# A fused attention and feed-forward kernel on one core: load order, one VectorE swap, and the weight preparations of fc, w2 and b2 on other queue places and engines

## The chip, the core and the metric

The kernel runs on 1 core of one Trainium2 chip. The metric is the time on the device in microseconds (us), the median of several runs. The engines of the core work from queues of their own, in order, and wait for one another by semaphores: TensorE (PE, and PEld for its weight loads), VectorE (DVE), ScalarE (ACT), GpSimd (POOL) and SyncE (SP, which only starts DMA transfers here).

## The reference

For x of 2 batches x 2048 rows x 128 columns, float32:

```python
x = x + layernorm(attn(layernorm(x)))
x = x + layernorm(ffn(layernorm(x)))

def attn(h):                        # one head of width 128
    q, k = rope(bf16(h @ Wq.T)), rope(bf16(h @ Wk.T))
    e = where(causal, exp(q @ k.T / sqrt(128)), 0)
    o = e.sum(-1)                   # one number for each row, no values
    return relu(o[..., None] @ fc1_w.T + fc1_b) @ fc2_w.T + fc2_b   # 1 -> 16 -> 128

def ffn(h):                         # 16 experts; the gates are constant
    ...                             # gate 1 holds all the weight
    return relu(h @ W1[1] + b1[1]) @ W2[1] + b2[1]                  # 128 -> 256 -> 128
```

## The kernel before

The 4096 rows are 8 groups of 512 (4 tiles of 128 rows), group 0 to 3 of batch 0, 4 to 7 of batch 1. The front (first layernorm, q, k, rope) runs over nine units: unit 0 and 1 are the halves of group 0, unit 2 is group 1, unit 3 is group 4, unit 4 is group 5, unit 5 is group 2, 6 is group 6, 7 is group 3, 8 is group 7. The middle (scores, exponentials, attention's net, first residual, hidden layer) and the output have units of a similar kind.

The whole schedule is written out by hand in one text, `STEPS`. Each word is a step with its unit, an engine letter where there is a choice (A ScalarE, D VectorE, P GpSimd) and after # the banks of PSUM that it uses. Each engine walks the text and does its own steps in that order, so a step that waits holds up all the steps behind it on the same engine. A bank can be written again only when the step that empties it is done. The steps that matter here:

- `load_*` on SyncE's queue (L331 for x, L312 for the weights of q and k, L314 to L316 the three transfers of fc, L322 w2).
- `stat1.n` on VectorE (L642, bn_stats, two tiles in one instruction), `eps1.n` (variance plus epsilon; L357 on VectorE and GpSimd, L614 on ScalarE), `rstd1.n` on GpSimd (a power, L505), `norm1.n` (rows times rstd, L351), `tr1.n` on TensorE (transposes, L727), `+tr1.n` (copy of the bank to SBUF, L521).
- `wqk.0` (L710) centers the weights of q and k by a matmul, `+wqk.0` takes them to SBUF; `q.n`, `k.n` on TensorE (L735), `+q.n`, `+k.n` the copies to bf16 (L521).
- `swap.n`: two transfers (L339, L340) that exchange the halves of q and k for the rotation; units 0 and 1 use a matmul `rot.n` (L745) instead. `cos.n`, `sin.n` (L386, L383 on GpSimd, L410 from PSUM), `rope.n` (L420): products and the sum, most on VectorE.
- `scores.b.j.s` (L761, masks L765), `exp.b.j.s` on ScalarE with the row sum (L569), `sum.b` (L367), `hT.b` (L772), `+hT.b` (L538), `fc2.b` (L789).
- Weights: `fc.0` copies attention's net over the partitions by two pairs of matmuls (L717, L718); `fcmean.0` (L574, L575) and `+fc.0` (L579) on ScalarE take off each row's mean; `fcspread.0` on GpSimd (L472, L476) makes the block form by two selects. `w2mean.0` (L584) and `w2.0` (L590) do the same for the output's weights W2, `b2mean.0` (L594) and `b2.0` (L598) for b2. fc2.2 needs fcspread, the y steps (L810) need w2, and the splitting of b2 needs b2.

Of the kernel before, what the change touches and what calls it, by code (L numbers as in the profile page):

```python
# [38 lines left out]
load_x.3 blank.9#7 blank.1.256#7 load_x.0 repeat.0 load_x.4 mask.0 load_wqk.0 load_fc.0 stat1.3 load_x.1 stat1.0  # L39
eps1.3.P load_x.6 eps1.0.D stat1.4 rstd1.0 wqk.0#0 load_x.2 rstd1.3 eps1.4.A norm1.0.D load_x.8 tr1.0#1 fc.0#2  # L40
+wqk.0.A rstd1.4 load_w2.0 stat1.1 +tr1.0.A norm1.3.D eps1.1.A load_x.5 fcmean.0 k.0#1 rstd1.1 norm1.4.D tr1.3#0
load_x.7 +fc.0 q.0#3 norm1.1.D +tr1.3.A load_table.1 fcspread.0 stat1.6 tr1.4#2 tr1.1#4 load_table.4 stat1.2 +tr1.4.A
q.3#0 load_b1.0 +tr1.1.A stat1.8 +k.0.A k.3#2 w2mean.0 load_table.0 eps1.6.D stat1.5 rstd1.6 +q.3.A k.1#1 load_table.2
load_b2.0 stat1.7 eps1.8.A k.4#4 +k.3.A rstd1.8 norm1.6.D +q.0.A swap.3 q.4#0 eps1.2.A +k.4.A rstd1.2 norm1.8.D
tr1.6#3 +q.4.A load_table.3 cos.3.D rot.0#4 tr1.8#2 +tr1.6.A swap.4 norm1.2.D q.1#0 +tr1.8.A q.6#3 cos.4.D eps1.5.A
w2.0 b2mean.0 b2.0 sin.3.D tr1.2#2 +k.1.A rstd1.5 k.6#5 rope.3.D +q.6.A +tr1.2.A cos.0.D scores.2.2.0#3 eps1.7.A
sin.0.D scores.2.3.0#1 exp.2.2.0 k.8#2 rstd1.7 sin.4.D exp.2.3.0 scores.2.0.0#3 rope.0.D scores.2.1.0#4 +k.6.A q.8#6
rope.4.D exp.2.1.0 swap.6 norm1.5.D +k.8.A k.2#5 exp.2.0.0 cos.6.D +q.8.A scores.3.2.0#12 sum.2.D +q.1.A
scores.0.1.0#3 cos.8.D swap.8 scores.3.3.0#67 exp.0.1.0 cos.1.P +k.2.D rot.1#0 exp.3.2.0 tr1.5#4 sin.1.D q.2#3
exp.3.3.0 +tr1.5.D norm1.7.P hT.2#0 scores.3.1.0#12 +q.2.D scores.3.0.0#45 +hT.2 sin.6.D q.5#6 exp.3.1.0 swap.2  # L50
rope.1.D scores.0.0.0#0 exp.3.0.0 rope.6.D scores.0.3.0#1 load_w1.0 fc2.2#23 exp.0.0.0 sin.8.D exp.0.3.0
scores.5.0.0#45 cos.2.D +q.5.A scores.5.3.0#01 rope.8.D exp.5.0.0 k.5#7 stat3.2.D scores.0.2.0#6 exp.5.3.0 sin.2.D
# [798 lines left out]
```

## Time and profile before

| | |
|---|---|
| time of three runs | 91.88 us median, 91.78 to 91.89 |
| the profiled execution | 91.72 us, of which the span of the instructions is 90.0 us |
| busy share of the span | PE 92%, PEld 55%, DVE 85%, ACT 79%, POOL 63% |
| chain that ended last, by engine | PE 67%, ACT 20%, DMA 4%, POOL 2% |
| granted TensorE clock, mean | 0.997 |

The profile is of one execution. Busy shares are averages over stages of different kinds; a matmul's record overlaps the next one's, so a busy PE is not one at its peak. The chain is followed back from the last instruction: at each step to what released it or to the instruction before it on its engine. A timeline row shows start, duration, engine, line, operation, result and inputs, count, and in brackets the idle time before it and what ended it.

### The profile page before, as it was taken

What the parts mean: (1) busy time and instruction counts of PE and PEld (TensorE: products, weight loads), DVE (VectorE), ACT (ScalarE), POOL (GpSimd) and SP (SyncE); (2) the same over time, 40 slices, a digit from 0 to 9 for tenths busy, and PEclk for the clock granted to TensorE, in tenths of its full rate; (3) what the DMA queues carried; (4) which work ended last, traced back from release to release, by engine and by line L of the source; (5) the groups of instructions that cost most, each with busy time, mean ns of one, the idle gap of its engine ahead of it and who ended that gap; (6) DMA issues with size and microseconds to landing.
All of it is one profiled execution on the core that took longest, in us unless ns stands there. A gap on an engine that the chain in (4) does not pass through costs nothing.

```text
span 90.0 us, 1535 instructions
## 1 busy us (share of the span) xinstructions
...
## 2 busy tenths in 40 slices
...
GB/s 26 244 240 277 312 294 170 205 15 87 149 63 123 0 117 0 60 60 0 0 0 7 0 0 0 0 0 0 53 64 11 0 120 0 0 25 149 179 246 101
DMA packets 11900, 7.64 MB, mean 85 GB/s; under 512 B 867, under 2 KB 10996, under 8 KB 11892
## 3 DMA queue, kind: packets, MB, share of 16 engines
...
q8 instruction: 3, 0.05, 0.2%
...
## 4 chain that ended last, share of the span: by engine, by line
PE 67%; ACT 20%; DMA 4%; POOL 2%; SPq 2%; issue 1%; POOLq 1%; DVE 0%
PE psum L735 24%; ACT psum L569 15%; PE psum L810 15%; PE psum L761 12%; PE psum L727 7%; DMA wqk_f<-wqk_t 4%; PE psum L789 3%; POOL rstd L505 2%; SPq L331 2%; PE psum L781 1%; ACT qk L521 1%; PE psum L710 1%; PE psum L765 1%; PE psum L772 1%; PE psum L800 1%
## 5 line engine op out<-in xcount | busy, mean ns | idle before, releaser
L505 POOL TENSOR_TENSOR rstd<-ve,half_neg 128x4 f32<-128x4 f32 (+2 forms) x38 | 34.8, 925 | 13.8 <-DVE ve L357 9.6
L569 ACT ACTIVATE psum<-psum 128x1024 f32<-128x1024 f32 (+7 forms) x48 | 36.7, 764 | 1.4 <-PE psum L761 0.6
L761 PE MATMUL psum<-qk_r 128*128 128x512 bf16 (+3 forms) x80 | 20.7, 349 | 1.4 <-ACT psum L569 0.6
L810 PEld LDWEIGHTS psum<-w_c,hid 128*128 128x128 f32 x128 | 15.6, 192 | 1.3 <-DVE cols_n L521 0.4
L735 PE MATMUL psum<-cols_n,wqk 128*128 128x512 f32 (+1 forms) x36 | 16.1, 556 | 0.0
L810 PE MATMUL psum<-w_c,hid 128*128 128x128 f32 x128 | 16.1, 278 | 0.0
L735 PE MATMUL psum<-cols_n,w_c 128*128 128x512 f32 (+1 forms) x36 | 15.6, 552 | 0.0
L761 PEld LDWEIGHTS psum<-qk_r 128*128 128x128 bf16 x80 | 6.6, 97 | 12.9 <-ACT psum L569 6.4
L727 PE MATMUL psum<-ident,rows_n 128*128 128x128 f32 x64 | 10.2, 277 | 0.1
L357 POOL TENSOR_SCALAR ve<-stats 128x4 f32<-128x4 f32 (+2 forms) x9 | 2.1, 233 | 11.6 <-DVE stats L642 6.6
L727 PEld LDWEIGHTS psum<-ident,rows_n 128*128 128x128 f32 x64 | 7.2, 141 | 3.8 <-issue 1.6
L614 ACT ACTIVATE ve<-stats,small 128x4 f32<-128x4 f32 (+1 forms) x12 | 3.6, 301 | 7.1 <-DVE stats L642 6.0
L569 ACT ACTIVATION_READ_ACCUMULATOR psum<-psum 128x1 f32 x48 | 9.2, 192 | 0.0
L675 DVE SCALAR_TENSOR_TENSOR x<-psum,rstd,x_s 128x128 f32<-128x128 f32 x32 | 9.0, 342 | 0.2
L642 DVE BATCH_NORM_STATS2 stats<-x_s 128x6 f32<-128x256 f32 x16 | 5.8, 418 | 3.5 <-DMA x_s<-x 3.5
L649 DVE BATCH_NORM_STATS2 stats<-psum 128x6 f32<-128x256 f32 x21 | 8.0, 420 | 0.8 <-PE psum L810 0.5
L621 ACT ACTIVATE rows_n<-psum 128x128 f32<-128x128 f32 x22 | 5.8, 278 | 3.2 <-PE psum L810 2.3
L735 PEld LDWEIGHTS psum<-cols_n,w_c 128*128 128x128 f32 x36 | 6.2, 191 | 3.6 <-issue 2.0
L383 POOL TENSOR_TENSOR qk_r<-qk,table 128x512 bf16<-128x512 bf16 (+1 forms) x6 | 6.1, 1043 | 2.5 <-issue 2.5
L735 PEld LDWEIGHTS psum<-cols_n,wqk 128*128 128x128 f32 x36 | 6.0, 190 | 2.4 <-issue 1.1
L521 ACT ACTIVATE cols_n<-psum 128x512 f32<-128x512 f32 (+1 forms) x11 | 5.8, 538 | 1.8 <-PE psum L727 1.5
L521 ACT ACTIVATE qk<-psum 128x512 bf16<-128x512 f32 (+1 forms) x13 | 6.6, 536 | 0.3 <-PE psum L735 0.3
...
## 6 DMA issues: line engine op xcount, KB each, us to landing
...
```

Of the source, the lines that this page charges most:

```text
L383: last = eng.tensor_tensor(dst[:, g, i, c], src[:, g, i, c], table[:, kind, t0:t0 + w], ALU.mult)
L505: ready[k].done(eng.tensor_tensor(rstd[:, g, STAT_SLOT[k], t], ve[:, g, STAT_SLOT[k], t], half_neg[:, 0:tiles], ALU.pow), n)
L521: return eng.activation(dst, src, ACT.Copy) if on_act else eng.tensor_copy(dst, src)
L569: exps.done(eng.activation(area, area, ACT.Exp, scale=scale_qk, accum_out=sums[:, g, s, j:j + 1]), n, j, s)
L621: ins = eng.activation(rows_n[:, g, j0 + j, :], area, ACT.Square, accum_out=squares(g, k, slice(j0 + j, j0 + j + 1)))
L642: ins = eng.bn_stats(pair_stats(g, k, j), source[:, g, j:j + 2, :].rearrange("p t c -> p c t"))
L649: ins = eng.bn_stats(pair_stats(g, k, j0 + j), net_pair(k, n, j))
L675: ins = eng.scalar_tensor_tensor(dst[:, g, j0 + j, :], area, rstd[:, g, STAT_SLOT[k], j0 + j:j0 + j + 1], prev[:, g, j0 + j, :], ALU.mult, ...
L727: mm = eng.transpose(bank[:, j * P:(j + 1) * P], rows_n[:, g, j0 + j, :], ident[:, :])
L735: made[name].done(eng.matmul(bank_of(name, n)[:, 0:tiles * P], weight, cols_n[:, g, c], start=True, stop=True), n)
L761: mm = eng.matmul(psum[:, own[0] + i, 0:width], query, qk_r[:, g0 + c, 1, 0:width], start=True, stop=c < gb)
L810: mm = eng.matmul(bank[:, j * P:(j + 1) * P], hid[:, g, h, (j0 + j) * P:(j0 + j + 1) * P], w2_c[:, h, :], start=not seeded and h == 0, sto ...
```

## The change

In engine order it does this:

- SyncE: `load_wqk` is third, ahead of `load_x.4`, instead of fourth; `load_fc` comes after `load_x.8` instead of after `load_wqk`, still ahead of `load_w2`.
- VectorE: `norm1.0` comes ahead of `stat1.4`; `w2mean.0` is new here, between `rope.0` and `rope.4`, as one bn_stats over both halves of W2 (128x256).
- TensorE: `fc.0` comes between `k.1` and `k.4`, in bank 6, instead of between `tr1.0` and `k.0`, in bank 2.
- ScalarE: `fcmean.0` and `+fc.0` come after `+k.4` instead of after `eps1.1`; `w2mean.0` and `w2.0` are gone; `b2mean.0` and `b2.0` come after `exp.2.0.0` instead of after `eps1.5`.
- GpSimd: `fcspread.0` comes after `rstd1.7` instead of after `rstd1.1`; `w2.0` is new here, after `norm1.7`: one subtraction of 128x256.

All other steps keep their order on each engine. In `STEPS` the text is wrapped anew; its beginning, and then the code:

```diff
-load_x.3 blank.9#7 blank.1.256#7 load_x.0 repeat.0 load_x.4 mask.0 load_wqk.0 load_fc.0 stat1.3 load_x.1 stat1.0
-eps1.3.P load_x.6 eps1.0.D stat1.4 rstd1.0 wqk.0#0 load_x.2 rstd1.3 eps1.4.A norm1.0.D load_x.8 tr1.0#1 fc.0#2
-+wqk.0.A rstd1.4 load_w2.0 stat1.1 +tr1.0.A norm1.3.D eps1.1.A load_x.5 fcmean.0 k.0#1 rstd1.1 norm1.4.D tr1.3#0
-load_x.7 +fc.0 q.0#3 norm1.1.D +tr1.3.A load_table.1 fcspread.0 stat1.6 tr1.4#2 tr1.1#4 load_table.4 stat1.2 +tr1.4.A
-q.3#0 load_b1.0 +tr1.1.A stat1.8 +k.0.A k.3#2 w2mean.0 load_table.0 eps1.6.D stat1.5 rstd1.6 +q.3.A k.1#1 load_table.2
-load_b2.0 stat1.7 eps1.8.A k.4#4 +k.3.A rstd1.8 norm1.6.D +q.0.A swap.3 q.4#0 eps1.2.A +k.4.A rstd1.2 norm1.8.D
-tr1.6#3 +q.4.A load_table.3 cos.3.D rot.0#4 tr1.8#2 +tr1.6.A swap.4 norm1.2.D q.1#0 +tr1.8.A q.6#3 cos.4.D eps1.5.A
-w2.0 b2mean.0 b2.0 sin.3.D tr1.2#2 +k.1.A rstd1.5 k.6#5 rope.3.D +q.6.A +tr1.2.A cos.0.D scores.2.2.0#3 eps1.7.A
-sin.0.D scores.2.3.0#1 exp.2.2.0 k.8#2 rstd1.7 sin.4.D exp.2.3.0 scores.2.0.0#3 rope.0.D scores.2.1.0#4 +k.6.A q.8#6
...
+load_x.3 blank.9#7 blank.1.256#7 load_x.0 repeat.0 load_wqk.0 load_x.4 mask.0 stat1.3 load_x.1 stat1.0 eps1.3.P
+load_x.6 eps1.0.D norm1.0.D stat1.4 rstd1.0 wqk.0#0 load_x.2 rstd1.3 eps1.4.A load_x.8 load_fc.0 tr1.0#1 +wqk.0.A
+rstd1.4 load_w2.0 stat1.1 +tr1.0.A norm1.3.D eps1.1.A load_x.5 k.0#1 rstd1.1 norm1.4.D tr1.3#0 load_x.7 q.0#3
+norm1.1.D +tr1.3.A load_table.1 stat1.6 tr1.4#2 tr1.1#4 load_table.4 stat1.2 +tr1.4.A q.3#0 load_b1.0 +tr1.1.A stat1.8
++k.0.A k.3#2 load_table.0 eps1.6.D stat1.5 rstd1.6 +q.3.A k.1#1 fc.0#6 load_table.2 load_b2.0 stat1.7 eps1.8.A k.4#4
++k.3.A rstd1.8 norm1.6.D +q.0.A swap.3 q.4#0 eps1.2.A +k.4.A fcmean.0 +fc.0 rstd1.2 norm1.8.D tr1.6#3 +q.4.A
+load_table.3 cos.3.D rot.0#4 tr1.8#2 +tr1.6.A swap.4 norm1.2.D q.1#0 +tr1.8.A q.6#3 cos.4.D eps1.5.A sin.3.D tr1.2#2
++k.1.A rstd1.5 k.6#5 rope.3.D +q.6.A +tr1.2.A cos.0.D scores.2.2.0#3 eps1.7.A sin.0.D scores.2.3.0#1 exp.2.2.0 k.8#2
+rstd1.7 fcspread.0 sin.4.D exp.2.3.0 scores.2.0.0#3 rope.0.D w2mean.0.D scores.2.1.0#4 +k.6.A q.8#6 rope.4.D exp.2.1.0
+swap.6 norm1.5.D +k.8.A k.2#5 exp.2.0.0 b2mean.0 b2.0 cos.6.D +q.8.A scores.3.2.0#12 sum.2.D +q.1.A scores.0.1.0#3
+cos.8.D swap.8 scores.3.3.0#67 exp.0.1.0 cos.1.P +k.2.D rot.1#0 exp.3.2.0 tr1.5#4 sin.1.D q.2#3 exp.3.3.0 +tr1.5.D
+norm1.7.P w2.0.P hT.2#0 scores.3.1.0#12 +q.2.D scores.3.0.0#45 +hT.2 sin.6.D q.5#6 exp.3.1.0 swap.2 rope.1.D
...
@@ -204,6 +204,7 @@
         b2_s = sb("b2_s", [P, P], BF16)
         ones_b = sb("ones_b", [P, P], BF16)
         means = sb("means", [P, 4], F32)
+        w2_stats = sb("w2_stats", [P, HC, 3], F32)
         spare = sb("spare", [P, 4, P], F32)
 
         x_s = sb("x_s", [P, n_groups, TILES, P], F32)
@@ -244,7 +245,7 @@
         exps, summed, biased = signal("exp", "act"), signal("sum", "dve"), signal("bias", "dve")
         x1_done, out_done = signal("x1", "dve"), signal("out", "dve")
         x1_scaled, out_scaled = signal("xs", "dve"), signal("ys", "dve")
-        mean_fc, mean_w2, w2_done = signal("fcmean", "act"), signal("w2mean", "act"), signal("w2", "act")
+        mean_fc, mean_w2, w2_done = signal("fcmean", "act"), signal("w2mean", "dve"), signal("w2", "pool")
         mean_b2, b2_done = signal("b2mean", "act"), signal("b2", "act")
         fc_spread = signal("fcspread", "pool")
         b2_split, b2_rows = signal("b2split", "pool"), signal("b2rows", "dve")
@@ -495,6 +496,11 @@
                     make_mask()
                 elif name == "fcspread":
                     spread_fc()
+                elif name == "w2":
+                    mean_w2.wait(eng, 0)
+                    w2_done.done(eng.tensor_tensor(w2_c[:, :, :], w2_f[:, :, :],
+                                                   w2_stats[:, :, 1].unsqueeze(2).to_broadcast([P, HC, P]),
+                                                   ALU.subtract), 0)
                 elif name == "repeat":
                     make_repeat()
                 elif name[0:4] == "rstd":
@@ -578,17 +584,6 @@
                     mean_fc.wait(eng, 0)
                     taken["fc"].done(eng.activation(fc2_c[:, :], bank_of("fc", 0)[:, P:2 * P], ACT.Identity,
                                                     bias=means[:, 2:3]), 0)
-                elif name == "w2mean":
-                    eng.wait_ge(l_w2, 16)
-                    for h in range(HC):
-                        ins = eng.activation(spare[:, h, :], w2_f[:, h, :], ACT.Copy, scale=-1.0 / P,
-                                             accum_out=means[:, h:h + 1])
-                    mean_w2.done(ins, 0)
-                elif name == "w2":
-                    mean_w2.wait(eng, 0)
-                    for h in range(HC):
-                        ins = eng.activation(w2_c[:, h, :], w2_f[:, h, :], ACT.Identity, bias=means[:, h:h + 1])
-                    w2_done.done(ins, 0)
                 elif name == "b2mean":
                     eng.wait_ge(l_b2, 16)
                     mean_b2.done(eng.activation(spare[:, 3, :], b2_f[:, :], ACT.Copy, scale=-1.0 / P,
@@ -676,6 +671,10 @@
                                                        rstd[:, g, STAT_SLOT[k], j0 + j:j0 + j + 1],
                                                        prev[:, g, j0 + j, :], ALU.mult, ALU.add)
                     (x1_done if k == 3 else out_done).done(ins, n)
+                elif name == "w2mean":
+                    eng.wait_ge(l_w2, 16)
+                    mean_w2.done(eng.bn_stats(w2_stats[:, :, :].rearrange("p h c -> p (h c)"),
+                                              w2_f[:, :, :].rearrange("p h o -> p o h")), 0)
                 elif name == "b2rows":
                     b2_split.wait(eng, 0)
                     eng.wait_ge(s_zero_b2, 1)
```

## Rows read from the trace of the kernel before

**Rows 1.** The chain in order of time: start us, us, what.

```profile
2.33 3.59 DMA wqk_f<-wqk_t
...
16.13 0.58 ACT w_c L590 x2
16.71 0.30 ACT spare L594 x2
...
17.04 0.40 ACT b_c L598
...
18.25 0.34 PE psum L761
```

**Rows 2.** Timeline of ScalarE, 4.8 to 24 us.

```profile
6.43 0.30 ACT L614 ACTIVATE ve<-stats,small 128x4 f32<-128x4 f32 x1 [4.36 <-DVE stats L642]
...
7.25 0.38 ACT L521 ACTIVATE cols_n<-psum 128x256 f32<-128x256 f32 x1
...
7.93 0.15 ACT L574 ACTIVATE fc<-psum 128x2 f32<-128x2 f32 x1
...
8.38 0.37 ACT L579 ACTIVATE fc_c<-psum,means 128x128 f32<-128x128 f32 x1
...
10.93 0.32 ACT L584 ACTIVATE spare<-w_f 128x128 f32<-128x128 f32 x1
...
13.28 0.60 ACT L521 ACTIVATE qk<-psum 128x512 bf16<-128x512 f32 x1
14.13 0.60 ACT L521 ACTIVATE qk<-psum 128x512 bf16<-128x512 f32 x1 [0.26 <-PE psum L735]
...
21.48 0.89 ACT L521 ACTIVATE qk<-psum 128x512 bf16<-128x512 f32 x2
22.55 0.37 ACT L569 ACTIVATE psum<-psum 128x256 f32<-128x256 f32 x1 [0.18 <-PE psum L765]
```

**Rows 3.** Timeline of VectorE, stretches between 5 and 24 us.

```profile
5.57 0.76 DVE L642 BATCH_NORM_STATS2 stats<-x_s 128x6 f32<-128x256 f32 x2 [0.46 <-DMA x_s<-x]
...
6.25 0.41 DVE L351 TENSOR_TENSOR rows_n<-x_s,rstd 128x256 f32<-128x256 f32 x1
7.27 0.43 DVE L642 BATCH_NORM_STATS2 stats<-x_s 128x6 f32<-128x256 f32 x1 [0.61 <-DMA x_s<-x]
...
8.88 0.86 DVE L351 TENSOR_TENSOR rows_n<-x_s,rstd 128x256 f32<-128x256 f32 x1
...
19.13 0.69 DVE L386 TENSOR_TENSOR qk_swap<-qk_swap,table 128x1024 bf16<-128x1024 bf16 x1 [0.37 <-DMA qk_swap<-qk]
...
22.18 0.69 DVE L386 TENSOR_TENSOR qk_r<-qk,table 128x1024 bf16<-128x1024 bf16 x1
```

**Rows 4.** Timeline of GpSimd, stretches between 6 and 30 us.

```profile
5.95 1.99 POOL L505 TENSOR_TENSOR rstd<-ve,half_neg 128x4 f32<-128x4 f32 x2
...
8.11 0.74 POOL L505 TENSOR_TENSOR rstd<-ve,half_neg 128x2 f32<-128x2 f32 x1 [0.17 <-ACT ve L614]
8.81 0.64 POOL L472 TENSOR_SCALAR_AFFINE_SELECT fc<-fc_c 128x512 f32<-128x512 f32 x1
...
22.50 1.53 POOL L383 TENSOR_TENSOR qk_r<-qk,table 128x256 bf16<-128x256 bf16 x2 [2.54 <-issue]
...
29.37 0.56 POOL L357 TENSOR_SCALAR ve<-stats 128x4 f32<-128x4 f32 x1 [4.34 <-DVE stats L649]
```

**Rows 5.** Timeline of TensorE, 4.8 to 24 us.

```profile
7.14 0.38 PE L717 MATMUL psum<-fc_f,repeat 17*128 17x2 f32 x2
7.38 0.46 PE L718 MATMUL psum<-fc_f,repeat 17*128 17x128 f32 x2
...
10.07 4.03 PE L735 MATMUL psum<-cols_n,wqk 128*128 128x512 f32 x10
...
16.88 1.02 PE L735 MATMUL psum<-cols_n,wqk 128*128 128x512 f32 x2
```

**Rows 6.** Busy time of each engine in the stretch 23 to 46 us.

```profile
23.00:46.00 23.00, 22.04 (x115) 10.44 (x113) 22.42 (x55) 22.91 (x60) 15.99 (x18) 1.00 0.23 53
```

42 lines of the change are left out of this document (21 added, 21 removed).

## The prediction

> **What bounds the kernel now.** I read the chain of waits first. After the start it lies on ScalarE from 16.13 to 18.21, on TensorE from 18.25, and on ScalarE's exponentials from 22.55 [rows 1, 2]. In it stand the very instructions that this change moves: the two of step `w2` (0.58), `b2mean` (0.30) and `b2` (0.40) [rows 1]. So at 16 to 18 us the chain has 1.28 us that no score needs, which looks like the gain. The timelines of the engines then say what else is close. TensorE runs the ten passes of q.3, k.3, k.1, k.4 and q.4 without a gap from 10.07, 4.03 us, and `+q.4` on ScalarE waits for the last of them at 14.13 after 0.26 us of idle [rows 2, 5]. TensorE's k.6 starts at 16.88 and lasts 1.02, its records overlapping [rows 5]; its end lies about 0.4 us before scores.2.2.0 begins at 18.25 [rows 1]. So 0.4 to 0.5 us is all that ScalarE's relief at 16 us can win before TensorE is the bound. VectorE is packed too: its only wait there is 0.37 us for the swapped half of unit 4 at 19.13 [rows 3].
>
> **The start.** The weights of q and k landed 3.59 us after an issue at 2.33 [rows 1], at 5.92. Issued one place sooner, 0.5 us, and ahead of a 256 KB block, they land between 4.7 and 5.4 (estimate: 5.92 less the issue, or less what the block took too). Then load_x.4 lands where the weights did, about 5.9 and not 5.5. The saving reaches `tr1.0` only if unit 0's rows are scaled sooner too. They are: rstd1.0 ends by about 5.97, since GpSimd's next one starts at 5.95 [rows 4], where norm1.0 before began at 6.25 behind stat1.4 [rows 3]; now 6.02 to 6.43. But what ended the wait for block 3, stat1.4, now comes behind it: two instructions in 0.76 us [rows 3], so 6.35 to 7.11 instead of 5.57 to 6.33. On ScalarE's queue eps1.4 stands ahead of `+wqk.0` and `+tr1.0`, and it waits for stat1.4. Before it ran at 6.43 [rows 2]; now at 7.21. Behind it `+wqk.0` and `+tr1.0` (0.30 for eps1.4, 0.38 each, partly overlapped) end at 8.1 where `+tr1.0` ended at 7.63 [rows 2]. So k.0 starts 0.4 to 0.6 us later than before, about 8.2. The reordering that was to free unit 0 holds it back through a third engine's queue.
>
> How much of that is left at q.3, where TensorE becomes continuous? Before, q.3 waited for norm1.1, a 128x256 product that began at 8.88 and took 0.86, against 0.41 for its like at 6.25 [rows 3]. After, eps1.4 ends at 7.51; GpSimd's rstd1.4 (1.0, half of the 1.99 of two) and rstd1.1 (0.71) end at 8.6 and 9.3 [rows 4]; norm1.1 runs 9.35 to 9.76. The fc steps have left TensorE and ScalarE here, and their 0.7 and 0.8 us were in a hole. k.0, tr1.3, q.0, tr1.4 and tr1.1 then end at 10.15. q.3 starts at 10.16 where it started at 10.07: the start gives nothing, minus 0.3 to plus 0.2. That blocks 1, 6, 2 and 8 are issued ahead of the three loads of fc wins at most the 0.61 us that VectorE waited before 7.27 [rows 3]; stat1.4 now fills most of it.
>
> **fc.** In its new place fc stands between k.1 and k.4, in TensorE's gapless stretch. Before, its two pairs of matmuls started at 7.14 and 7.38 [rows 5]: 0.48 us by the distance of the pairs, 0.7 by the stretch up to the next one's end. I take 0.5. So `+k.4`, at 13.28 before [rows 2], comes at about 13.85. Then ScalarE does fcmean and `+fc`, from 7.93 to 8.75 in the old place [rows 2], 0.7 us with the next overlapped, and `+q.4` starts at about 15.05 instead of 14.13: 0.9 late, since only 0.26 of idle was there. Behind it: swap.4's two transfers, `+tr1.6`, `+tr1.8`, eps1.5. The old w2mean (two of 0.32 and their reads, from 10.93 [rows 2]) gives 0.6 back, but at a place where ScalarE then waits for TensorE.
>
> **w2 and b2.** With w2, b2mean and b2 gone from 16.03, `+k.1` comes at 16.7 and `+q.6` at 17.3, when TensorE has finished q.6. Now TensorE's order decides: tr1.6 to k.6 took 13.94 to 17.8 without waits and starts 0.5 to 0.6 late, so k.6 ends at 18.35 to 18.4 and scores.2.2.0 starts at 18.4 instead of 18.25: 0.15 late (0.05 early if fc costs 0.3). The 1.28 us are gone, 0.5 to fc on TensorE, the rest to the idle time of ScalarE. Then b2mean and b2 come back behind exp.2.0.0: 0.70 to 0.73 us. `+q.8` and `+q.1` started at 21.48 [rows 2] and now start at 22.35; exp.0.1.0, at 22.55 after 0.18 of idle, now starts at 23.1: 0.57 late. VectorE's cos.8 started at 22.18 right behind `+q.8` [rows 2, 3]; now it can't before 23.05, 0.89 late. Behind it in VectorE's queue stand `+k.2` and sin.1, whose end lets hT.2 into bank 0, and ScalarE waits for hT.2; by the timeline that way has 0.2 to 0.3 us of slack. So the shift on ScalarE is 0.57 by its own queue, 0.6 to 0.7 by VectorE. From 23 to 46 us ScalarE is busy 22.91 of 23.00 us [rows 6], and TensorE takes over from it: nothing gives the time back.
>
> **w2 elsewhere.** w2mean on VectorE is one 128x256 bn_stats, 0.43 by rows 3, 0.36 in a full queue; with swap.4 0.9 late (its landing may catch up, since traffic ahead of it is less: sin.4 from 0.2 early to 0.9 late) VectorE is 0.4 to 1.3 late at rope.4, which is near the 0.89 that cos.8 sets anyway. If nothing were late there, it would cost 0.36. GpSimd's w2, below 1.1 and likely 0.6 us, lies in its 4.34 us of idle before 29.37 [rows 4], and y.2 needs it after 50 us: nothing; without that cover 0.6. fcspread, 0.64 and about 0.70, falls in GpSimd's 2.54 us of idle before 22.50 [rows 4]: nothing for GpSimd itself. But the first select, 8.81 to 9.45, lay on norm1.1, which took 0.45 us more than its like [rows 3, 4]. At 20 to 21.3 us it now meets rope sums and norm1.5. I take nothing of it into the sum, since VectorE has about 0.5 us before cos.8's new start to lose, and keep 0 to 1.3 for the range.
>
> The Trainium skill, SBUF — State Buffer, Terms, says that VectorE and GpSimd arbitrate for a shared port pair that is held for the full instruction, so that "the loser fully blocks". The trace agrees at norm1.1, 0.86 beside 0.41. By the rule alone both selects would come off VectorE's time; by my sum neither does.
>
> **Sum.** Start 0.1, fc on TensorE 0.5, less 0.4 to 0.45 of the hole before scores.2.2.0, makes 0.15; b2's 0.73 less 0.18 of idle and the overlap, 0.42, makes 0.57; VectorE's way adds 0.1. That is 0.7 us (0.4 to 1.0). The profiled execution has a span of 90.0 and took 91.72, so 92.4; it lies 0.16 below the median of the three runs, 91.88, and against that the forecast is 92.6.
>
> **Rivals.** (1) Forecast, 52%: 92.6, 92.3 to 92.9. (2) VectorE becomes the bound, 17%: the two selects hold it, 1.3 us, of which 0.5 is slack, or swap.4 lands late; it decides once VectorE's delay at cos.8 exceeds 0.9. Then 0.5 to 0.8 more, 93.2. For it: 0.86 at norm1.1. Against it: it is one instance, and which engine wins a tie can't be seen. The page's rule stands beside this one: it is that rule at its full price. (3) Faster, 18%: TensorE is not what sets 10 to 18 us, because the fc passes and late k.4 fit into waits that its overlapping records hide. Then ScalarE counts alone: it loses 0.6 for w2mean and 0.58 for w2 and gains 0.8 for fc, 0.4 net, and exp.0.1.0 comes that much sooner: 91.5. It decides if `+k.4` is less than 0.2 us late. Against it: ten passes in 4.03 us [rows 5], without a gap. (4) No change that can be told, 13%: the delay is there, 0.4 to 0.7, but is given back between 23 and 46 because the exponentials had been waiting more than the profile shows: 91.9.
>
> What this kernel's measurement can tell from no change is 0.2%, 0.18 us. Slower is (1) and (2), 69%; same is (4), 13%; faster is (3), 18%. The range goes from 91.6, which leaves out about 12 in 100 of (3), to 93.2, which leaves out half of (2); the forecast's own range is 92.3 to 92.9.
>
> **What would show it.** Right: eps1.4 on ScalarE at about 7.2 and k.0 at 8.2; q.3 near 10.2; `+k.4` near 13.85 and `+q.4` near 15.0 with fcmean between; scores.2.2.0 near 18.4; exp.0.1.0 near 23.1 and cos.8 at 23. Wrong: k.0 before 7.8, scores.2.2.0 before 18.0, or cos.8 at 22.2. Products of two tensors on VectorE that take over 0.8 us near 20 would be (2). What makes me wrong most easily is the start: a quarter of a microsecond there, either way, goes through the whole kernel.

## The result, and the profile after

The changed kernel took 94.88 us, the median of five executions (95.0, 93.16, 94.88, 96.19, 93.58), against 91.89 for the kernel before (91.78 to 93.08 beside it). In three of the five, the mean granted TensorE clock was 0.956 to 0.982; in the two where it was 1.0, the change took 93.16 and 93.58. Of these the ratio is 1.0186 (95% interval 1.0141 to 1.0232). Ratios and intervals, here and below, leave out executions that a low clock made longer, as far as nothing else is said. The kernel is slower, on the side forecast; 92.6 was too low, and the median lies outside the range, which ended at 93.2.

The profile is of the execution of 95.0 us (span 93.3). Its chain of waits begins otherwise than [rows 1]: the sums of block 4 and k.0 stand in it (start us, us, what).

```profile
2.33 4.10 DMA x_s<-x
6.45 0.77 DVE stats L637 x2
...
8.21 1.22 PE psum L734 x2
```

TensorE's timeline:

```profile
6.55 0.41 PE L726 MATMUL psum<-ident,rows_n 128*128 128x128 f32 x2 [0.18 <-DVE rows_n L352]
8.21 1.22 PE L734 MATMUL psum<-cols_n,wqk 128*128 128x256 f32 x2 [1.25 <-ACT cols_n L527]
...
11.89 2.31 PE L734 MATMUL psum<-cols_n,wqk 128*128 128x512 f32 x6
14.13 0.38 PE L716 MATMUL psum<-fc_f,repeat 17*128 17x2 f32 x2
...
14.77 1.99 PE L734 MATMUL psum<-cols_n,wqk 128*128 128x512 f32 x4
```

Busy time in stretches (PE, PEld, DVE, ACT, POOL, then the granted clock, DMA share, GB/s), the last one for [rows 6]:

```profile
7.50:8.00 0.50, 0.00 (x0) 0.00 (x0) 0.50 (x2) 0.50 (x3) 0.31 (x1) 1.00 1.09 302
8.00:8.50 0.50, 0.29 (x1) 0.30 (x2) 0.13 (x1) 0.34 (x2) 0.50 (x1) 0.63 1.19 310
8.50:10.00 1.50, 1.50 (x6) 1.21 (x6) 0.97 (x2) 0.00 (x0) 1.16 (x2) 0.50 1.15 299
10.00:11.50 1.50, 1.50 (x7) 1.21 (x6) 1.50 (x6) 0.60 (x1) 0.00 (x0) 0.50 1.16 296
...
23.00:46.00 23.00, 21.18 (x101) 9.70 (x102) 22.42 (x53) 22.51 (x58) 15.07 (x19) 1.00 0.30 64
```

From the end of `tr1.0` to k.0 TensorE is empty for 1.25 us, where the matmuls of fc stood before [rows 5]. From about 8.2 to 11.5 us the granted clock is 0.50, the lower of the two levels (1.2 of 2.4 GHz), and k.0's two passes take 1.22 us. q.3 starts at 11.89, not at 10.07.

ScalarE's timeline, beside [rows 2]:

```profile
7.31 0.30 ACT L609 ACTIVATE ve<-stats,small 128x4 f32<-128x4 f32 x1 [5.24 <-DVE stats L637]
...
7.78 0.37 ACT L527 ACTIVATE cols_n<-psum 128x256 f32<-128x256 f32 x1
...
15.93 0.60 ACT L527 ACTIVATE qk<-psum 128x512 bf16<-128x512 f32 x1 [1.07 <-PE psum L734]
...
20.95 0.47 ACT L575 ACTIVATE psum<-psum 128x384 f32<-128x384 f32 x1 [0.25 <-PE psum L764]
```

The start of it is as foretold: eps1.4 at 7.31 holds `+wqk.0` and `+tr1.0` back, and k.0 starts at 8.21. What the low clock then costs was in no term of the sum. So the first experiment gives the change at the full clock, and the other readings of where the time went are made on that.

### The profile page after: what moved, and what is told of

Read it like the earlier page. It is cut to its first block, busy times and chain, and to the rows that moved or that the text cites. A ratio compares the mean times of both kernels' runs of the same rounds, so it can differ in the third digit from the quotient of the medians.

```text
span 93.3 us, 1525 instructions
## 1 busy us (share of the span) xinstructions
PE 84.4 (91%) x439; PEld 50.9 (55%) x444; DVE 78.0 (84%) x203; ACT 69.8 (75%) x204; POOL 58.8 (63%) x84
## 4 chain that ended last, share of the span: by engine, by line
PE 58%; ACT 13%; DVE 11%; DMA 8%; issue 2%; SPq 2%; POOL 2%; POOLq 1%; DVEq 0%; ACTq 0%
PE psum L734 22%; PE psum L809 14%; ACT psum L575 9%; PE psum L760 7%; PE psum L726 7%; DMA x_s<-x 4%; DMA qk_swap<-qk 3%; PE psum L788 3%; DVE qk_swap L387 3%; DVE qk L527 3%; POOL rstd L511 2%; DVE qk_r L421 2%; ACT qk L527 2%; PE psum L780 1%; SPq L332 1%
## 5 line engine op out<-in xcount | busy, mean ns | idle before, releaser
L511 POOL TENSOR_TENSOR rstd<-ve,half_neg 128x4 f32<-128x4 f32 (+2 forms) x38 | 35.7, 948 | 17.1 <-DVE ve L358 11.0
L760 PE MATMUL psum<-qk_r 128*128 128x512 bf16 (+3 forms) x75 | 19.9, 346 | 1.8 <-ACT psum L575 0.8
L734 PE MATMUL psum<-cols_n,wqk 128*128 128x512 f32 (+1 forms) x36 | 17.4, 591 | 1.2 <-ACT cols_n L527 1.2
L726 PE MATMUL psum<-ident,rows_n 128*128 128x128 f32 x64 | 10.7, 290 | 0.2 <-DVE rows_n L352 0.2
L726 PEld LDWEIGHTS psum<-ident,rows_n 128*128 128x128 f32 x64 | 8.3, 152 | 3.7 <-issue 2.1
L352 DVE TENSOR_TENSOR rows_n<-x_s,rstd 128x512 f32<-128x512 f32 (+1 forms) x8 | 5.4, 674 | 2.7 <-POOL rstd L511 2.7
```

The source lines that it names most:

```text
L352: normed[k].done(eng.tensor_tensor(rows_n[:, g, t, :], (x_s if k == 1 else x1)[:, g, t, :], scale, ALU.mult), n)
L511: ready[k].done(eng.tensor_tensor(rstd[:, g, STAT_SLOT[k], t], ve[:, g, STAT_SLOT[k], t], half_neg[:, 0:tiles], ALU.pow), n)
L726: mm = eng.transpose(bank[:, j * P:(j + 1) * P], rows_n[:, g, j0 + j, :], ident[:, :])
L734: made[name].done(eng.matmul(bank_of(name, n)[:, 0:tiles * P], weight, cols_n[:, g, c], start=True, stop=True), n)
L760: mm = eng.matmul(psum[:, own[0] + i, 0:width], query, qk_r[:, g0 + c, 1, 0:width], start=True, stop=c < gb)
```

## The experiments

Each was timed in turn with the kernel before, which had medians of 91.76 (17 executions, beside runs 1 to 4), 91.81 (24, beside 5 to 8), 92.44 (24, beside 9 to 12) and 91.83 (25, beside 13 to 16). "Late" and "sooner" are against the profile before. Each profile is of one execution, and loads land some tenths earlier or later in each: with the start of the kernel before, q.3 begins at 10.07 (before), 10.09 (run 4), 9.49 (7), 10.21 (8) and 9.96 (12). All kernels compute the whole reference; `blank.n` is n idle matmuls of 512 columns (of 256 where it says so) that nothing reads. Diffs show the place in the written order.

**1. The change, with four idle matmuls in TensorE's hole.**

```diff
-load_fc.0 tr1.0#1 +wqk.0.A
+load_fc.0 tr1.0#1 blank.2#7 blank.2.256#7 +wqk.0.A
```

> The change with four short blank matmuls (two of 512 columns, two of 256) put into TensorE's hole between tr1.0 and k.0; nothing else differs. Theory (the hole that the change opened lets the clock fall in most executions): the granted clock stays 1.00 from 5 to 15 us, k.0 takes 0.6 and not 1.2 us, and all runs lie at 93.1 to 93.6, none near 95. Rival (the clock falls by chance, whatever TensorE does there): three runs in five stay at 94.9 to 96. If the blanks only delay k.0: 93.6 to 94.

93.4 us (93.34 to 93.59), ratio 1.0191 (1.016 to 1.0221); the mean granted clock was 1.0 in all five executions. TensorE's, ScalarE's, VectorE's and GpSimd's timelines follow, beside [rows 5, 2, 3] and [rows 4]:

```profile
8.20 0.70 PE L734 MATMUL psum<-cols_n,wqk 128*128 128x256 f32 x2 [0.32 <-ACT cols_n L527]
...
10.48 2.31 PE L734 MATMUL psum<-cols_n,wqk 128*128 128x512 f32 x6
12.72 0.38 PE L716 MATMUL psum<-fc_f,repeat 17*128 17x2 f32 x2
...
13.36 1.98 PE L734 MATMUL psum<-cols_n,wqk 128*128 128x512 f32 x4
15.18 0.60 PE L726 MATMUL psum<-ident,rows_n 128*128 128x128 f32 x4
...
19.13 0.33 PE L760 MATMUL psum<-qk_r 128*128 128x384 bf16 x1
```

```profile
14.52 0.60 ACT L527 ACTIVATE qk<-psum 128x512 bf16<-128x512 f32 x1 [1.06 <-PE psum L734]
...
15.74 0.59 ACT L527 ACTIVATE qk<-psum 128x512 bf16<-128x512 f32 x1
...
19.55 0.47 ACT L575 ACTIVATE psum<-psum 128x384 f32<-128x384 f32 x1 [0.24 <-PE psum L764]
...
23.74 0.38 ACT L575 ACTIVATE psum<-psum 128x256 f32<-128x256 f32 x1
...
28.58 0.58 ACT L575 ACTIVATE psum<-psum 128x512 f32<-128x512 f32 x1 [0.24 <-PE psum L764]
...
29.75 1.01 ACT L575 ACTIVATE psum<-psum 128x1024 f32<-128x1024 f32 x1
```

```profile
9.02 1.09 DVE L352 TENSOR_TENSOR rows_n<-x_s,rstd 128x512 f32<-128x512 f32 x2 [0.90 <-POOL rstd L511]
...
21.23 1.13 DVE L352 TENSOR_TENSOR rows_n<-x_s,rstd 128x512 f32<-128x512 f32 x1
22.29 1.12 DVE L387 TENSOR_TENSOR qk_r<-qk,table 128x1024 bf16<-128x1024 bf16 x1
...
23.66 0.69 DVE L387 TENSOR_TENSOR qk_r<-qk,table 128x1024 bf16<-128x1024 bf16 x1
...
26.67 0.96 DVE L387 TENSOR_TENSOR qk_swap<-qk_swap,table 128x1024 bf16<-128x1024 bf16 x1
```

```profile
7.68 1.98 POOL L511 TENSOR_TENSOR rstd<-ve,half_neg 128x4 f32<-128x4 f32 x2 [0.81 <-ACT ve L609]
...
20.88 0.94 POOL L473 TENSOR_SCALAR_AFFINE_SELECT fc<-fc_c 128x512 f32<-128x512 f32 x1
21.89 0.97 POOL L477 TENSOR_SCALAR_AFFINE_SELECT fc<-fc 128x512 f32<-128x512 f32 x1
...
26.47 0.61 POOL L501 TENSOR_TENSOR w_c<-w_f,w_stats 128x256 f32<-128x256 f32 x1
```

k.0 starts where it did in the change, but takes 0.70 us, and q.3 comes at 10.48 instead of 11.89. These 1.41 us are nearly all of the 1.6 between 95.0 and 93.4. What is left, 1.64 us over the median of 91.76 (1.75 by the ratio), is the change's price at the full clock, and these rows are its account.

**2. The change, eps1.4 behind `+tr1.0` on ScalarE.**

```diff
-eps1.4.A load_x.8 load_fc.0 tr1.0#1 ... +tr1.0.A norm1.3.D
+load_x.8 load_fc.0 tr1.0#1 ... +tr1.0.A eps1.4.A norm1.3.D
```

> The change with eps1.4 moved behind +wqk.0 and +tr1.0 on ScalarE. Theory (eps1.4's wait for stat1.4 holds +tr1.0, and with it k.0): k.0 starts at 7.4 to 7.5 instead of 8.2, the hole shrinks to half, the clock falls seldom or never, and tr1.4 still waits for norm1.4 until 9.5; time 93.0 to 93.5 with no run near 95. Rival (k.0 is held by something else): k.0 stays at 8.2 and the times at 93.2 to 96.

93.42 (93.22 to 93.58), ratio 1.0187 (1.0156 to 1.0218), clock at least 0.993 in all six. TensorE:

```profile
7.18 0.70 PE L734 MATMUL psum<-cols_n,wqk 128*128 128x256 f32 x2 [0.51 <-ACT cols_n L527]
...
9.87 0.88 PE L726 MATMUL psum<-ident,rows_n 128*128 128x128 f32 x6 [0.50 <-DVE rows_n L352]
```

k.0 is 1.0 sooner than in run 1, without a blank, and none of the six was long. But q.3 starts at 10.58 all the same, behind VectorE's rows: k.0's delay behind eps1.4 costs nothing at the full clock. Whether it is what brings the low clock, six executions against the change's five can't settle.

**3. The change, with all of fc at its old places.**

```diff
-tr1.0#1 +wqk.0.A ... k.1#1 fc.0#6 ... +k.4.A fcmean.0 +fc.0 ... rstd1.7 fcspread.0
+tr1.0#1 fc.0#2 +wqk.0.A ... eps1.1.A fcmean.0 +fc.0 ... rstd1.1 fcspread.0 ... k.1#1 ... +k.4.A ... rstd1.7
```

> The change with fc back in its old places: load_fc behind load_x.4, fc.0 between tr1.0 and k.0 in bank 2, fcmean and +fc behind eps1.1, fcspread behind rstd1.1. Theory (fc costs 0.5 us in TensorE's gapless stretch, 0.7 on ScalarE, and its selects hold VectorE at 22 to 24 us): 92.2 to 92.7, with fc's matmuls in the hole the clock falls less often, and VectorE's norm1.5 and cos.6 take 0.69 us again, not 1.1. Rival (the loss is in the start and in b2): 93.2 or more.

At a clock of 0.992 or more 92.27, 92.35, 92.53 and 92.53; at 0.973 and 0.974: 93.39 and 93.6. The ratio, 1.0119 (1.0067 to 1.017), counts all six. By the four, fc costs 0.9 to 1.1 within the change. The clock is low in two of six although fc's matmuls are back in the hole. The profile, one of the longer executions, shows VectorE:

```profile
21.45 0.69 DVE L352 TENSOR_TENSOR rows_n<-x_s,rstd 128x512 f32<-128x512 f32 x1
22.06 0.68 DVE L387 TENSOR_TENSOR qk_r<-qk,table 128x1024 bf16<-128x1024 bf16 x1
...
23.66 0.69 DVE L387 TENSOR_TENSOR qk_r<-qk,table 128x1024 bf16<-128x1024 bf16 x1 [0.78 <-issue]
```

Without a select beside them, norm1.5 and cos.6 take 0.69 and 0.68 instead of 1.13 and 1.12. But cos.8 then stands idle for 0.78 us, since `+q.8` comes no sooner behind b2. The selects' hold of 0.9 us is there and is hidden.

**4. Before, with w2mean, w2, b2mean and b2 moved alone.**

```diff
-k.3#2 w2mean.0 ... eps1.5.A w2.0 b2mean.0 b2.0 sin.3.D ... rope.0.D ... exp.2.0.0 ... norm1.7.P
+k.3#2 ... eps1.5.A sin.3.D ... rope.0.D w2mean.0.D ... exp.2.0.0 b2mean.0 b2.0 ... norm1.7.P w2.0.P
```

> The kernel before with only w2mean on VectorE, w2 on GpSimd, and b2mean and b2 behind exp.2.0.0. Theory of the prediction: scores.2.2.0 up to 0.4 us sooner, exp.0.1.0 about level, so 91.6 to 92.1. Rival (b2 behind exp.2.0.0 holds +q.8 and so cos.8, and this is a main part of the loss): 92.4 or more.

92.16 (91.56 to 95.07, twelve executions), ratio 1.0031 (1.0005 to 1.0057). exp.2.2.0 comes at 18.40, 0.35 sooner, as the prediction's step at 16 us says; b2 uses that up, and exp.0.1.0 starts at 22.59, 0.04 late. Then ScalarE waits 0.25 at 27.43, and the next full exponential comes at 28.61, 0.51 late. VectorE's sin.6, which is ahead of that wait:

```profile
25.52 0.97 DVE L387 TENSOR_TENSOR qk_swap<-qk_swap,table 128x1024 bf16<-128x1024 bf16 x1
```

It took 0.68 before. GpSimd's w2 stands beside it (25.33 to 25.94). Its price was not nothing.

**5. Before, with the start alone** (the load of the weights third, norm1.0 ahead of stat1.4).

```diff
-load_x.4 mask.0 load_wqk.0 ... eps1.0.D stat1.4 ... eps1.4.A norm1.0.D
+load_wqk.0 load_x.4 mask.0 ... eps1.0.D norm1.0.D stat1.4 ... eps1.4.A
```

> The kernel before with the start alone: load_wqk third and norm1.0 ahead of stat1.4; fc, w2 and b2 as before. Theory: stat1.4 ends late, eps1.4 holds +wqk.0 and +tr1.0, and GpSimd's rstd1.4 then runs beside norm1.3 and takes 1.3 instead of 1.0 us, so q.3 starts 0.2 to 0.4 us late and ScalarE's chain with it: 91.9 to 92.2. Rival (the start is neutral, as the prediction had it within 0.1): 91.6 to 91.85.

92.02 (91.81 to 93.12, twelve), ratio 1.0054 (1.0021 to 1.0087). It counts two executions at a clock of 0.973 and 0.981 (93.1 and 93.12); by the other ten the start costs 0.3 to 0.4. q.3 starts at 10.31, 0.24 late, and the exponentials from 18 to 31 us are all 0.25 late.

**6. Before, with fc alone moved.**

```diff
-load_fc.0 stat1.3 ... fc.0#2 ... fcmean.0 k.0#1 ... +fc.0 ... fcspread.0 ... k.1#1 ... +k.4.A ... rstd1.7
+stat1.3 ... load_x.8 load_fc.0 ... k.0#1 ... k.1#1 fc.0#6 ... +k.4.A fcmean.0 +fc.0 ... rstd1.7 fcspread.0
```

> The kernel before with fc alone in its new places: load_fc behind load_x.8, fc.0 between k.1 and k.4, fcmean and +fc behind +k.4, fcspread behind rstd1.7. Theory: 0.7 us more in TensorE's gapless stretch and 0.7 on ScalarE, where w2, b2mean and b2 still stand, so scores.2.2.0 is 0.9 to 1.1 us late: 92.6 to 92.9. Rival (fc costs the 0.15 that the sum of the prediction left of it): 91.9 to 92.1. The two selects should make norm1.5 and cos.6 on VectorE 1.1 us long each.

Two groups: 92.33 to 92.6 (four executions) and 93.91 to 94.24 (five). The shorter ones have a ratio of 1.0075 (1.0044 to 1.0106). The profile is of the longer group. TensorE:

```profile
6.12 1.19 PE L710 MATMUL psum<-wqk_f,center 128*128 128x256 f32 x2 [0.64 <-DMA wqk_f<-wqk_t]
...
8.21 1.22 PE L735 MATMUL psum<-cols_n,wqk 128*128 128x256 f32 x2 [0.47 <-ACT cols_n L521]
```

Two passes of 256 columns that take 0.67 and 0.70 before take 1.19 and 1.22, although the granted clock reads 1.00 in this stretch. The first of them lies ahead of the hole that fc left: in this execution TensorE was slow already at 6.12 and had not become fast by 8.21, so the hole did not slow it. Five of nine are long here, against 5 of 24 of the kernel before beside it, which is too few to say that fc's removal does it.

**7. As 4, with w2 straight behind w2mean on GpSimd.**

```diff
-rstd1.7 ... norm1.7.P w2.0.P
+rstd1.7 ... w2mean.0.D w2.0.P ... norm1.7.P
```

> The kernel with only the w2 and b2 parts (d_w2b2_only), but GpSimd's w2 straight behind rstd1.7, so that it runs at 20 us and not at 25 to 26 beside sin.6. Theory (GpSimd's subtraction holds VectorE's two-input product sin.6 for 0.3 us and rope.1, exp.0.3.0 with it): sin.6 takes 0.68 instead of 0.97, exp.0.3.0 does not wait, and 91.4 to 91.7 against 91.9 to 92.1 of d_w2b2_only. Rival (the 0.4 us are lost elsewhere): 91.9 to 92.1 again.

92.05 (91.61 to 94.46, twelve), ratio 1.0034 (1.0006 to 1.0062, with one of 92.79 at a clock of 0.973): as 4. GpSimd and VectorE:

```profile
20.28 2.33 POOL L501 TENSOR_TENSOR w_c<-w_f,w_stats 128x256 f32<-128x256 f32 x1 [1.09 <-ACT qk L527]
```

```profile
21.31 0.68 DVE L387 TENSOR_TENSOR qk_r<-qk,table 128x1024 bf16<-128x1024 bf16 x1
```

The subtraction that took 0.61 takes 2.33 behind VectorE's products (rope.4 from 20.12, norm1.5, cos.6 to 21.99), which lose nothing; it ends at 22.61, 0.62 after the last of them. sin.6 is back at 0.68. From exp.2.2.0 to the exponential that run 4 has at 28.61 it takes 9.92 us instead of 10.21. But exp.2.2.0 itself came at 18.55, 0.15 later than in run 4, so half of that was gone.

**8. As 7, with b2mean and b2 at their old place.**

```diff
-w2mean.0.D w2.0.P ... exp.2.0.0 b2mean.0 b2.0
+eps1.5.A b2mean.0 b2.0 ... w2mean.0.D w2.0.P ... exp.2.0.0
```

> As w_w2_early, but b2mean and b2 in their old place behind eps1.5, where ScalarE now has 0.24 and 0.45 us of idle before +q.6 and exp.2.2.0. Theory (b2 behind exp.2.0.0 costs 0.4 to 0.7 because it stands in front of +q.8 and cos.8): exp.2.2.0 at 18.4 to 18.5 as before but exp.0.1.0 at 22.1 to 22.3, time 91.1 to 91.5, faster than the kernel before by 0.4 us. Rival (TensorE or VectorE is the bound there): 91.5 to 91.9.

A miss: 93.09 (92.16 to 94.48, six), ratio 1.0114 (1.0068 to 1.016). It was to be faster than both kernels. VectorE:

```profile
22.59 0.69 DVE L368 COPY osum<-sums 128x128 f32<-128x128 f32 x1
23.20 1.17 DVE L387 TENSOR_TENSOR qk_r<-qk,table 128x1024 bf16<-128x1024 bf16 x1
```

GpSimd's w2 (20.54, 0.99) meets norm1.5 (20.97, 1.10 for 0.69), and its cos.1 (22.52) meets the copy of the sums, 0.21 to 0.22 in runs 1, 3, 4 and 7, and cos.8.

**9. The change, with fc's load and its four matmuls back, the rest of fc late.**

```diff
-load_x.8 load_fc.0 tr1.0#1 +wqk.0.A ... k.1#1 fc.0#6
+stat1.3 load_fc.0 load_x.1 ... tr1.0#1 fc.0#6 +wqk.0.A ... k.1#1
```

> The change with only fc's matmuls and their load in the old place (load_fc behind load_x.4, fc.0 between tr1.0 and k.0, still in bank 6); fcmean, +fc and fcspread stay in the new places. Theory: TensorE's stretch from q.3 to q.4 loses its 0.7 us of fc, +k.4 comes 0.7 sooner, and the 0.7 on ScalarE stays: 92.7 to 93.0 against 93.4. The hole before k.0 holds four matmuls again, so the clock falls seldom. Rival (it is fcmean and +fc on ScalarE, or the selects, that cost, TensorE's part is hidden): 93.2 to 93.5.

At a clock of 0.993 or more 92.3, 92.34, 92.98 and 93.46, at 0.981 93.74 and 93.91; ratio 1.0117 (1.0052 to 1.0181). TensorE, one of the longer executions:

```profile
8.21 1.22 PE L734 MATMUL psum<-cols_n,wqk 128*128 128x256 f32 x2 [0.54 <-ACT cols_n L527]
...
11.71 4.03 PE L734 MATMUL psum<-cols_n,wqk 128*128 128x512 f32 x10
15.58 0.60 PE L726 MATMUL psum<-ident,rows_n 128*128 128x128 f32 x4
```

The ten passes are in one piece again, 3.87 us to `tr1.6`; with fc between them it was 4.70 (run 1). The times spread too widely to split fc's price finely, but two of the four are as low as run 3's. With fc's matmuls back, TensorE waits 0.54 us and not 1.25 before k.0, and k.0 still takes 1.22.

**10. The change, with b2mean and b2 at their old place.**

```diff
-eps1.5.A sin.3.D ... exp.2.0.0 b2mean.0 b2.0
+eps1.5.A b2mean.0 b2.0 sin.3.D ... exp.2.0.0
```

> The change with b2mean and b2 in their old place behind eps1.5. Theory of the prediction (b2 behind exp.2.0.0 costs 0.4 to 0.6 us by holding +q.8): exp.0.1.0 0.4 to 0.7 sooner and times of 92.8 to 93.0 where the clock holds. Rival (after g_b2_old_place: with +q.8 and +q.1 sooner, GpSimd's cos.1 meets VectorE's norm1.5 or cos.8 and one of them is held): 93.3 or more.

94.1 (93.85 to 96.57, six), ratio 1.0251 (1.0215 to 1.0286): the four at a clock of 0.995 or more took 93.85 to 94.11, 0.6 more than run 1. The other two took 95.38 and 96.57. TensorE, VectorE, GpSimd and ScalarE:

```profile
8.44 0.70 PE L734 MATMUL psum<-cols_n,wqk 128*128 128x256 f32 x2 [1.24 <-ACT cols_n L527]
```

```profile
23.55 0.71 DVE L368 COPY osum<-sums 128x128 f32<-128x128 f32 x1
24.18 1.17 DVE L387 TENSOR_TENSOR qk_r<-qk,table 128x1024 bf16<-128x1024 bf16 x1
```

```profile
23.51 1.30 POOL L384 TENSOR_TENSOR qk_r<-qk,table 128x256 bf16<-128x256 bf16 x2 [0.42 <-issue]
```

```profile
23.62 0.37 ACT L575 ACTIVATE psum<-psum 128x256 f32<-128x256 f32 x1 [0.25 <-PE psum L764]
...
26.98 0.46 ACT L544 ACTIVATE h1T<-psum,fc 128x128 f32<-128x128 f32 x1 [0.93 <-PE psum L771]
```

exp.0.1.0 comes only 0.12 sooner than in run 1, because VectorE, beside two selects (norm1.5 1.12, cos.6 1.11), is late, and cos.1 on GpSimd now starts before cos.8 and holds it. ScalarE pays 0.93 at hT.2. This is the second rival, in a kernel other than the change. In the row of TensorE the change's hole is there, 1.24 us, and k.0 takes the 0.70 us of the full clock behind it.

**11. Before, with only the load of fc behind `load_x.1`.**

```diff
-mask.0 load_wqk.0 load_fc.0 stat1.3 load_x.1
+mask.0 load_wqk.0 stat1.3 load_x.1 load_fc.0
```

> The kernel before with one word moved: load_fc behind load_x.1 instead of ahead of it. Theory (block 1's landing, for which VectorE waits 0.6 us at 7.27, sets norm1.1 and the start of q.3): stat1.1 0.4 to 0.6 sooner, q.3 0.2 to 0.5 sooner, 91.4 to 91.6. Rival (fc's own load then comes late and holds k.0, or swap.3's landing sets rope.3): 91.7 to 92.1.

Two groups again: six executions at 91.3 to 92.2, six at 93.38 to 94.87; ratio of the first 0.9997 (0.9961 to 1.0033). In the profile (93.5) TensorE waits 0.86 us for the weights of q and k and 0.42 for fc's rows, and k.0 runs at half the clock (8.24, 1.22). But of the kernel before, beside it, 12 of 24 were long as well, so the fall says nothing on this edit. stat1.1 starts at 6.57, 0.7 sooner, and no time is gained.

**12. Before, with two more idle matmuls ahead of the weights.**

```diff
-load_x.3 blank.9#7 blank.1.256#7 load_x.0
+load_x.3 blank.9#7 blank.1.256#7 blank.2#7 load_x.0
```

> The kernel before with two more blank matmuls of 512 columns at the end of the first ones, so that TensorE is busy to about 5.7 and not to 4.85. Theory (the executions of the kernel before at 93 to 94.7 are those in which TensorE's rate is low after 5 us, because it had been idle for 1.2 us there): all executions at 91.6 to 92.0, none over 92.5. Rival (the rare long executions have another cause): one in five still over 92.7.

91.75 (91.42 to 92.13, twelve), ratio 1.0003 (0.9976 to 1.0029). None of the twelve is long, while beside it 12 of the 24 executions of the kernel before took 92.8 to 95.0. So the kernel before has the long executions too, and two idle matmuls ahead of the weights take them away.

**13. As 1, with w2 later on GpSimd, behind rstd3.2.**

```diff
-norm1.7.P w2.0.P ... rstd3.2
+norm1.7.P ... rstd3.2 w2.0.P
```

> a_blanks (the change with blanks in the hole, so at the full clock) with GpSimd's w2 moved from behind norm1.7 to behind rstd3.2, four to five us later. Theory: at 26.5 us it held VectorE's sin.6 for 0.3 us, and rope.1 and exp.0.3.0 behind it, which ScalarE then waited for; away from there sin.6 takes 0.68 us, ScalarE does not idle at 28.3, and the time is 93.0 to 93.15 against 93.4. If the subtraction holds another product on VectorE's way, it stays at 93.3 to 93.5. Rival (the idle at 28.3 comes from elsewhere): it stays although sin.6 is short.

93.52 (93.39 to 93.56), ratio 1.0162 (1.0121 to 1.0202). sin.6 takes 0.68 and ScalarE has no wait: 9.93 us from exp.2.2.0 to the exponential of 29.59, against 10.20 in run 1. But the time was to be 93.0 to 93.15: the 0.27 is lost again later. w2 now stands ahead of cos.5 on GpSimd (32.59, 0.70); which wait takes it was not isolated.

**14. Before with fc moved (as 6), holes filled.**

```diff
-blank.1.256#7 load_x.0 ... tr1.0#1 +wqk.0.A
+blank.1.256#7 blank.2#7 load_x.0 ... tr1.0#1 blank.3.256#7 +wqk.0.A
```

> The kernel before with fc alone in its new places and blank matmuls before wqk and between tr1.0 and k.0, so that the clock holds. Theory: no execution near 94; the clean price of fc is 0.6 to 1.0 us, 92.4 to 92.8, of which 0.7 stand on TensorE between k.1 and k.4. Rival (the second group of times of f_fc_only has nothing to do with TensorE's idle time): 92.4 and 94 again.

92.51 (92.25 to 92.84, twelve), ratio 1.0071 (1.0051 to 1.009), and the group near 94 is gone; with blanks in two places it can't be told which of them does it, but runs 12 and 16 do it with the first alone. q.3 starts at 9.88, k.4 0.64 after fc, and scores.2.2.0 at 19.00, 0.75 late, although q.3 is 0.19 sooner: ScalarE still has w2 and b2 ahead of `+q.6` here.

**15. As 1, with stat1.4 ahead of norm1.0 again.**

```diff
-eps1.0.D norm1.0.D stat1.4 rstd1.0
+eps1.0.D stat1.4 norm1.0.D rstd1.0
```

> a_blanks with stat1.4 ahead of norm1.0 again on VectorE, all else as changed. Theory (with load_x.4 behind the weights, block 4's rows land at 5.9 to 6.4, so either order ends stat1.4 near 7.1): norm1.0 ends 0.6 to 0.7 later, +tr1.0 waits for it and not for eps1.4, k.0 at 8.4 to 8.6, but q.3 is set by norm1.4 and norm1.1 and moves by 0.1 or less: 93.2 to 93.5, no change against 93.4. Rival (scaling unit 0 first is the part that helps): 93.7 or more. Rival (it is the part that hurts): 93.1 or less.

At a clock of 0.994 or more 93.58 to 93.83, at 0.98 and 0.979 95.08 and 94.96; ratio 1.0211 (1.0153 to 1.0269, with the one of 94.96). norm1.0 starts at 7.05, norm1.1 at 9.93 instead of 9.69. With the block's load already late, scaling unit 0 first helps by 0.2 to 0.4 us, where no change was expected. TensorE here waits 1.33 us ahead of `tr1.0`, and the blanks behind it don't keep two of six from the low clock.

**16. Before as in 12, with the load of fc issued by ScalarE.**

```diff
-load_x.3 blank.9#7 blank.1.256#7 load_x.0 ... load_wqk.0 load_fc.0
+load_fc.0.A load_x.3 blank.9#7 blank.1.256#7 blank.2#7 load_x.0 ... load_wqk.0
```

> The kernel before with two more blank matmuls before wqk, and the three loads of fc issued from ScalarE's queue instead of SyncE's, which brings block 1's load 1.1 us forward without delaying fc. Theory (block 1's landing sets norm1.1 and so q.3 and swap.3): q.3 0.3 to 0.5 sooner, 91.2 to 91.5. Rival (swap.3's transfer then lands among the other loads and sets rope.3 as before): 91.6 to 91.9.

91.88 (91.37 to 92.28, twelve), ratio 1.0008 (0.9983 to 1.0032). stat1.1 starts at 6.66 instead of 7.27, three transfers less being issued ahead of its block, but nothing is left of the gain. GpSimd's powers stand beside VectorE's products (three in 3.68 us from 11.29, where before they took 2.96 from 11.89); that this is what takes it is read from the rows and not tested.

## Why the prediction was wrong, step by step

At the full clock (run 1), its sum can be set beside the measured one, each against the profile before:

| | predicted | run 1 |
|---|---|---|
| q.3, the start | +0.1 | +0.41 (10.48 for 10.07) |
| fc on TensorE, q.3 to `tr1.6` | +0.5 | +0.83 (4.70 for 3.87) |
| less the hole before scores.2.2.0 | -0.4 to -0.45 | -0.36 (3.95 for 4.31) |
| scores.2.2.0 | +0.15 | +0.88 (19.13 for 18.25) |
| b2 behind exp.2.0.0 | +0.42 | +0.39 (from +0.80 at exp.2.2.0 to +1.19 at exp.0.1.0) |
| VectorE's way and GpSimd's w2, to 29.75 | +0.1 | +0.46 (29.75 for 28.10, +1.65) |

So two things failed: the clock had no term, and three terms of the sum were too small. The terms alone put run 1 at 93.4, outside the range; the clock takes the change's median on to 94.88.

**The clock was left out.** It is the largest miss: 1.41 us at q.3 in the profile, with a mean clock of 0.956 to 0.982 in three of five executions. The step that failed is "The fc steps have left TensorE and ScalarE here, and their 0.7 and 0.8 us were in a hole", as far as it makes an emptier TensorE cost nothing. The prediction had k.0 at 8.2 and `tr1.0` done by 7, so the hole could be read off it, but no term and no rival asked what the clock would do. That the low clock is what costs this is shown: in run 1 k.0 starts at the same time and q.3 comes 1.41 sooner.

What makes the clock low is not shown, and it is not fc's leaving alone. Call an execution long if its mean clock is below 0.985 or its time over 1.5% above the kernel's fastest. With the hole open (the change and run 10) 5 of 11 are long, and run 10's profile has a hole of 1.24 us without a fall. With fc's matmuls back in it (runs 3 and 9) 4 of 12 are long. With idle matmuls there, none of 10 (runs 1 and 13) and 2 of 6 (run 15); with k.0 sooner, none of 6 (run 2). The kernel before, which has no hole there, is long in 3 of 17, 5 of 24, 12 of 24 and 3 of 25. The one clear difference is that of the idle matmuls ahead of the weights: none of 36 (runs 12, 14 and 16). So the change may have made the low clock more frequent, but these counts don't prove it, and the kernel that would settle it, the change with the idle matmuls of run 12, was not run.

The Trainium skill, TensorE: Matmul & The Clock Gate, Part 1: The HAM clock gate (the "warmup" mystery), says that the array is throttled by default and that activity releases it. The trace agrees for the start of the kernel: the first ten idle matmuls, 4864 columns, took 3.52 to 4.24 us in the runs' profiles, and run 1's four later ones, 1536 columns, 0.81 us, 0.72 to 0.87 ns for a column against 0.53.

**The start was mis-sized: 0.41, not 0.1.** eps1.4 at 7.3 and k.0 at 8.2 came as forecast. But rstd1.4 was priced at "1.0, half of the 1.99 of two", and it took 1.31 us, started while VectorE's norm1.3 ran; so norm1.1 starts at 9.69, not 9.35. This 0.34 goes through to q.3. In run 2, k.0 is 1.0 sooner and q.3 no sooner, which shows that VectorE and GpSimd set it and not ScalarE's queue. The sentence that the reordering holds unit 0 back "through a third engine's queue" names a true delay of k.0 that the time at the full clock doesn't pay. The late load of fc has a part in it, which the prediction counted as a small gain: with that load in its old place VectorE waits for block 1 (runs 3 and 5: 0.58 and 0.54 us), norm1.3 comes later, and rstd1.4 and rstd1.1 take 1.68 and 1.67 together; with it late there is no such wait, and they take 1.98 (the change, runs 1 and 2).

**fc on TensorE was mis-sized: 0.83, not 0.5.** The distance of the old pairs, 0.48 us, is what they took in idle time, and not between passes of 512 columns. The other reading that the prediction gave, 0.7, was the better one: 0.64 from fc to k.4, and 0.19 more up to `tr1.6`, whose cause no run isolates. In run 9, without fc there, it is 3.87 again, and in run 14, with fc alone moved, 4.70.

**The hole before scores.2.2.0 was right.** Run 4 wins 0.35 at exp.2.2.0 by w2 and b2 alone, and run 1 has 0.36 of it. It was set against 0.6 us, and the true delays of start and fc came to 1.24. At the exponential of 28.10 the three parts alone are 0.26 (start, run 5), 0.76 (fc, run 14) and 0.51 late (w2 and b2, run 4), 1.53 together, and the whole is 1.65 late: they nearly add up. By times, the start costs 0.3 to 0.4, w2 and b2 0.3, fc 0.7 (runs 6 and 14), 1.3 to 1.4 together, against 1.64 to 1.75 of the whole, and the intervals of each, 0.2 to 0.3 us either way, leave open whether this is more than their sum.

**b2 was right in size, and its place is not a loss within the change.** Put back, the kernel gets 0.6 slower (run 10) and not faster. By run 10's rows, b2's 0.7 us on ScalarE keep `+q.1` behind VectorE's delays, and so cos.1 on GpSimd behind cos.8.

**"Nothing" for GpSimd's w2 was wrong in kind.** Its 0.61 us do lie in idle time of GpSimd, but sin.6 on VectorE takes 0.96 for 0.68 beside it, and ScalarE waits 0.24 behind that. Runs 7 and 13, against 4 and 1, show 0.29 and 0.27 at this place, of the 0.46 of the last row; the other 0.19 was not isolated. Moving w2 away wins no time that can be told (runs 7, 13).

**The rivals.** The second is half true. The selects do hold VectorE, twice 0.44 us: 0.88 of their 1.91. The prediction took the rule of the Trainium skill (SBUF — State Buffer, Terms) to mean that their whole length comes off VectorE's time, 1.3 us. The rows fit the rule if the one that comes second waits for the rest of the other's instruction: norm1.5 starts at 21.23 and the first select ends at 21.82, cos.6 at 22.29 and the second at 22.86. The selects lose by it too, 0.94 and 0.97 for 0.64 and 0.70. But in the change VectorE is behind `+q.8` anyway (run 3: idle for 0.78 without the selects). It becomes the bound in runs 8 and 10. The third and fourth fell: `+k.4` was 1.24 late, and the 1.19 of exp.0.1.0 grew to 1.65 instead of being given back; ScalarE is busy 22.66 of 23.00 us from 24.5 to 47.5 in run 1.
